# Reordering a step of an attention loop: output matmuls dealt out among scores and attention, transposes between the two value tiles

## What is computed

```python
h_q = (x @ w_q.T).reshape(b, lq, H, DH)
h_k = (key_value_states @ w_k.T).reshape(b, lk, H, DH)
h_v = (key_value_states @ w_v.T).reshape(b, lk, H, DH)
score = jnp.einsum('bqhd,bkhd->bhqk', h_q, h_k)
score = score + position_bias[None]
m = attention_mask[:, None]
score = jnp.where(m, score, -jnp.inf)
score = jax.nn.softmax(score, axis=-1)
score = jnp.where(m, score, 0.0)
attn = jnp.einsum('bhqk,bkhd->bqhd', score, h_v).reshape(b, lq, H * DH)
out = attn @ w_out.T
```

## Time and profile before

| | |
|---|---|
| runs of the kernel before | 1075.21, 1072.99, 1074.5 us; median 1074.5 |
| profiled execution: span | 1071.4 us (the page gives no other time of this execution) |
| PE busy | 1037.1 us, 97% |
| PEld busy | 903.5 us, 84% |
| DVE, ACT, POOL busy | 659.0, 458.9, 313.4 us |
| chain that ended last | PE 88%, DVE 5%, POOL 2%, ACT 2% |
| PE waiting for probabilities (line 1463) | 5.5 us, 2 times, longest 4.2 |
| PE waiting for their split (line 1336) | 4.5 us, 3 times, longest 1.6 |

### The profile page before, as it was taken

The page is one execution under the profiler, slowest core; times in us unless marked ns, Lnnn a source line. Parts: engine busy times, 40 slices in busy tenths (PEclk is TensorE's granted clock), DMA queues, the critical chain, the costliest instruction groups (busy, mean ns, idle before and its releaser), DMA issues.

```text
span 1071.4 us, 16826 instructions
## 1 busy us (share of the span) xinstructions
PE 1037.1 (97%) x5946; PEld 903.5 (84%) x5946; DVE 659.0 (62%) x1189; ACT 458.9 (43%) x1090; POOL 313.4 (29%) x236
## 2 busy tenths in 40 slices
PE   8989999999999999999999999999999999799995
PEld 7778888888888888888888888888888888578784
DVE  5766666666666666666666666666666666853615
ACT  6866343434343434343434343434343434254251
POOL 1645040404040404040404040404040402343204
PEclk9999999999999999999999999999999999899998
DMA  9402020202020202020202020202020300300011
GB/s 299 134 1 84 2 84 1 83 0 83 0 83 0 83 0 83 0 83 0 83 0 83 0 83 0 83 0 83 0 83 0 122 1 20 109 21 1 1 40 40
DMA packets 20698, 52.39 MB, mean 49 GB/s; under 512 B 3136, under 2 KB 7232, under 8 KB 20672
## 3 DMA queue, kind: packets, MB, share of 16 engines
q1 hardware_dynamic: 20672, 52.06, 14.6%
HBM read 49.95 MB, written 2.10 MB: 49 GB/s over the span
## 4 chain that ended last, share of the span: by engine, by line
PE 88%; DVE 5%; POOL 2%; ACT 2%; issue 1%; DMA 1%; DVEq 0%; SPq 0%; POOLq 0%; ACTq 0%
PE psum L1330 25%; PE psum L1332 25%; PE psum L1331 25%; PE psum L1336 8%; PE psum L1337 3%; PE psum L1463 3%; DMA raw<-in_dft 1%; POOL rows L511 1%; DVE st L1045 0%; PE psum L1568 0%; DVE wts L1012 0%; POOL stat L581 0%; DVE rsum L1240 0%; ACT xn_hi L647 0%; POOL stat L583 0%
## 5 line engine op out<-in xcount | busy, mean ns | idle before, releaser
L539 POOL TENSOR_TENSOR smx<-far,bias 128x512 f32<-128x512 f32 x64 | 82.7, 1292 | 423.2 <-DVE smx L1068 421.5
L735 ACT ACTIVATE smx<-smx,nmax 128x128 f32<-128x128 f32 x256 | 99.8, 391 | 231.8 <-DVE nmax L1074 231.8
L976 DVE TENSOR_TENSOR qk<-psum,qk 128x512 fp32r<-128x512 f32 x136 | 93.2, 687 | 105.1 <-ACT qk L647 105.1
L1330 PE MATMUL psum<-wv_lo,cx_hi 128*128 128x256 f32 x512 | 149.7, 292 | 0.3 <-DVE xn_lo L976 0.3
L1332 PE MATMUL psum<-wv_hi,cx_hi 128*128 128x256 f32 x512 | 144.5, 282 | 0.0
L1331 PE MATMUL psum<-wv_hi,cx_lo 128*128 128x256 f32 x512 | 144.5, 282 | 0.0
L647 ACT ACTIVATE qk<-psum 128x512 fp32r<-128x512 f32 x136 | 80.8, 596 | 140.7 <-PE psum L1332 140.6
L976 DVE TENSOR_TENSOR vv_lo<-psum,vv_hi 128x512 fp32r<-128x512 f32 x64 | 44.2, 691 | 124.9 <-ACT vv_hi L647 124.9
L489 POOL TENSOR_TENSOR wqk_lo<-raw,wqk_hi 128x1024 fp32r<-128x1024 f32 x31 | 74.3, 2396 | 127.8 <-ACT wqk_hi L647 127.8
L1330 PE MATMUL psum<-wo_lo,at_hi 128*128 128x512 f32 x256 | 105.9, 414 | 1.1 <-issue 1.1
L1330 PE MATMUL psum<-cx_lo,wqk_hi 128*128 128x512 f32 x256 | 100.3, 392 | 1.8 <-DVE wqk_lo L976 1.8
(11 more groups left out here) (184 smaller groups left out, 2351.7 us busy)
## 6 DMA issues: line engine op xcount, KB each, us to landing
raw<-in_wqk SPq DMA_DIRECT2D x32, 512.0 KB, 3.4
raw<-in_wv SPq DMA_DIRECT2D x16, 512.0 KB, 4.3
raw<-in_wo SPq DMA_DIRECT2D x16, 512.0 KB, 3.3
raw<-in_ffn SPq DMA_DIRECT2D x10, 512.0 KB, 3.3
raw<-in_dft SPq DMA_DIRECT2D x7, 512.0 KB, 4.6
acc<-in_x SPq DMA_DIRECT2D x2, 1024.0 KB, 9.1
raw<-in_ctxT SPq DMA_DIRECT2D x4, 512.0 KB, 10.2
bias<-in_bias SPq DMA_DIRECT2D x32, 64.0 KB, 1.8
```

What stands on the lines that cost most here:

```text
L539: nc.gpsimd.tensor_tensor(bm, far[:, HB * hf:HB * hf + HB, :], g_, ALU.add).then_inc(s_bm_ready, 1)
L735: a.activation(exps[:, b, :], scores_sb[:, b, :], ACT.Exp, bias=nmax[:, 1, b:b + 1], accum_out=esum[:, 0, b:b + 1]).then_inc(s_exp_done, 1)
L976: return v.tensor_tensor(dst, src, hi, ALU.subtract)
L1330: mm(out, lhs(0), rhs(1), start=first, stop=False)
```

## The change

PE's order in a step becomes: `project`, the first value tile, `turn_probs`, the second value tile, then the scores of step n + 1 with the six matmuls of the first output tile between them, then the attention of step n with the six of the second output tile between them. The waits of scores and of the first output bank stand ahead of the first block, those of attention and of the second bank ahead of the second. DVE follows: `softmax_in`, first `add_out`, `attended`, `softmax_out`, second `add_out`. ACT, POOL and SP keep their order. The number of instructions is the same. Step 0 keeps its order, step 1 has no outputs (its scores come ahead of its attention), step 62 has no values, step 63 is as before. `mm3` moves from lines 1330 to 1332 to lines 1333 to 1335, other lines likewise.

```diff
             every_pair(dve, pair_dve)
...
-                    attended(n, j)
                     if is_first(g) and j == 0:
+                        attended(n, j)
                         xt_lo(4)
                         xt_lo(5)
-                    if front:
                         softmax_in(n + 1)
...
+                    elif is_first(g) and j == 1:
+                        softmax_in(n + 1)
+                        attended(n, j)
+                        softmax_out(n + 1)
+                    elif last and j == 3:
+                        attended(n, j)
+                    else:
+                        softmax_in(n + 1)
+                        add_out(n - 2, 0, (2 * ((j + 2) % 4)) % B)
+                        attended(n, j)
+                        if last and j == 2:
+                            ffn_lo(UP[3])
+                        softmax_out(n + 1)
+                        add_out(n - 2, 1, (2 * ((j + 2) % 4) + 1) % B)
...
+            def scores_and_output(n, o, first_tile):
+
+                scores_ready(n)
+                output_bank(o, 0)
+                score_hi(0)
+                output_term(o, first_tile, 0, 0)
+                score_lo(0)
+                output_term(o, first_tile, 0, 1)
+                score_hi(1)
+                output_term(o, first_tile, 0, 2)
+                score_lo(1)
+                output_term(o, first_tile, 0, 3)
+                score_hi(2)
+                output_term(o, first_tile, 0, 4)
+                score_lo(2)
+                score_hi(3)
+                output_term(o, first_tile, 0, 5)
+                score_lo(3)
...
+            def attend_and_output(n, g, j, o, first_tile):
+
+                attend_ready(n, g, j)
+                output_bank(o, 1)
+                attend_hi(j, 0)
+                output_term(o, first_tile, 1, 0)
+                attend_lo(j, 0)
...
             def pair_pe(g):
...
-                    turn_probs(n)
-                    if not (last and j >= 2 or is_first(g) and j == 0):
-                        values(n + 2, g + (j >= 2), (2 * j + 4) % B)
-                    attend(n, g, j)
                     if is_first(g) and j == 0:
+                        turn_probs(n)
+                        attend(n, g, j)
                         transposes(HB)
                         transposes(HB + 1)
-                    if front:
                         scores(n + 1)
...
+                    elif last and j == 3:
+                        outputs(n - 2, g, 2)
+                        turn_probs(n)
+                        attend(n, g, j)
+                    else:
+                        if last and j == 2:
+                            turn_probs(n)
+                        else:
+                            values(n + 2, g + (j >= 2), tile)
+                            turn_probs(n)
+                            value_tile(tile, 1)
+                        if is_first(g) and j == 1:
+                            scores(n + 1)
+                            attend(n, g, j)
+                        else:
+                            outputs_ready(n - 2, g - (j < 2), tile)
+                            scores_and_output(n + 1, n - 2, tile)
+                            attend_and_output(n, g, j, n - 2, tile)
```

More of the change, by code:

```diff
@@ L1436, in values, with value_tile, score_hi, score_lo @@
                     pe.wait_ge(s_o_add, 2 * m - 8)
[L1437 to L1444, removed]
+                value_tile(first_tile, 0)
+            def value_tile(first_tile, i):
+                tk = slice((first_tile + i) * P, (first_tile + i + 1) * P)
+                for c in range(DC):
+                    last = mm3(psV[:, i * 2 * P:(i + 1) * 2 * P], lambda i_: cx[i_][:, c, tk],
+                               lambda i_: wv[i_][:, c, :], c == 0, c == DC - 1)
+                if i == 1:
+                    last.then_inc(s_v_mm, 1)
+            def score_hi(b):
+                bk = slice(b * P, (b + 1) * P)
+                mm(psS[:, b], qk[0][:, 0, bk], qk_parts[:, :, 1, bk], start=True, stop=False)
+            def score_lo(b):
+                bk = slice(b * P, (b + 1) * P)
+                last = mm(psS[:, b, 1], qk[1][:, 0, bk], qk[0][:, 1, bk], start=False, stop=True)
+                if b == HB - 1:
+                    last.then_inc(s_scores_mm, 1)
+            def scores_ready(n):
                 pe.wait_ge(s_q_lo, n + 1)
@@ L1450, in scores @@
                     pe.wait_ge(s_stats_a, HB + 1)
+            def scores(n):
+                scores_ready(n)
                 for b in range(HB):
[L1452 to L1454 removed]
+                    score_hi(b)
+                    score_lo(b)
             def turn_probs(n):
@@ L1474, in attend, with outputs_ready @@
                     pe.wait_ge(s_general, 2)
+            def attend(n, g, j):
+                attend_ready(n, g, j)
                 for b in range(HB):
[L1476 to L1480, removed]
+                    attend_hi(j, b)
+                    attend_lo(j, b)
+            def outputs_ready(o, g, first_tile):
                 hf = first_tile // HB
@@ L1488, in outputs, with output_bank @@
                     pe.wait_ge(s_a_lo, 4 * g + 2 + 2 * hf)
-                for i in range(2):
[L1490 to L1507, removed]
+            def output_bank(o, i):
+                if isinstance(o, int) and o in LATE:
+                    pe.wait_ge(s_q_lo, units)
+                    pe.wait_ge(s_k_lo, units)
+                    pe.wait_ge(s_scores_full, units)
+                    pe.wait_ge(s_o_add, 2 * (o - 2) + i + 1)
+                else:
+                    if i == 0:
+                        pe.wait_ge(s_k_lo, min(o + 4, units) if isinstance(o, int) else o + 4)
+                    else:
+                        pe.wait_ge(s_v_lo, min(o + 5, units) if isinstance(o, int) else o + 5)
+                    if isinstance(o, int) and due(2 * (o - 1) + i + 1):
+                        pe.wait_ge(s_o_add, 2 * (o - 1) + i + 1)
@@ new lines, in output_term, with outputs @@
+            def output_term(o, first_tile, i, k):
+                hf, tile, hp = first_tile // HB, (first_tile + i) % HB, k // 3
+                lhs, rhs = ((0, 1), (1, 0), (0, 0))[k % 3]
+                last = mm(out_banks(o)[i][:, :], at[lhs][:, hf, hp, tile * P:(tile + 1) * P], wo[rhs][:, hp, :],
+                          start=k == 0, stop=k == 5)
+                if k == 5:
+                    last.then_inc(s_o_mm, 1)
+            def outputs(o, g, first_tile):
+                outputs_ready(o, g, first_tile)
+                for i in range(2):
+                    output_bank(o, i)
+                    for k in range(6):
+                        output_term(o, first_tile, i, k)
```

51 lines of the change are left out of this document (30 added, 21 removed).

## The result

The changed kernel takes **1080.05 us** (median of 4 runs, 1079.42 to 1080.78) against 1073.74 us of the kernel before in the same session: a ratio of 1.0058, 95% interval 1.0041 to 1.0075. So it is slower by 0.6%, three times what can be told from no change. The forecast of 1075 us has this time in its range (1067 to 1083), but its sum missed by 5 us and the likeliest case, "same", did not happen.

What follows compares the result with a forecast made beforehand. TensorE was taken as the bound, busy 1037.1 of 1071.4 us. Terms -1.3 (step 2), 0 (loop) and +1.9 (end) summed to +0.6 us; with 3.1 us carried over from span to median, 1075 us, range 1067 to 1083.

Steps and rivals of the forecast that it cites:

- same: Whole kernel: time within 0.2% of the kernel before, given a chance of 0.47.
- The -1.3 us of step 2: Transposes between the two value tiles: the first tile fills PE's 1.29 us wait for probabilities in step 2.
- the three distances: Loop step: output add 1.25 us to spare, value split 0.8 us, key split done long before; no new wait, 0.
- loads hidden: Rival: loads behind low parts are fetched during the output before, 21.5 us less, 1053 us; chance 0.13.
- The end: Last pair of heads: last transposes move by +0.7 or +3.1 us, depending on POOL's third split; middle +1.9 taken.
- The high end: Upper range limit, 1083 us: forecast with +3.1 at the end, the clock's 4.2 us and small case of slow outputs.
- nothing in the rows decides between them: Last pair: whether DVE's next small operation precedes POOL's third split, probabilities ready at 918.2 or 920.6 us.
- the first term: Output matmuls dealt among scores and attention, 61 steps: taken as zero, at best 4.3 us less.
- the prediction's own sign: Loop step: forecast is wrong if the 13.38 us period moves by more than 0.035 us, since 61 make 0.2%.
- outputs slow beside short matmuls: Rival: dealt outputs beside 128-column matmuls cost more; 3.7 us, 1079 us, or 12.8 us, 1088 us; chance 0.18.
- the 0.235 by which I wanted to know it: Sign of slow outputs: more than 0.235 us per output matmul instead of 0.2325 us.
- The clock: Stretch at 1.2 GHz after the wait before the last transposes: 0 taken, bounds 4.2 us either way.

Runs made afterwards that it cites:

- e1: Changed kernel with the twelve output matmuls back in one piece behind attention, other reordering kept; 1072.86 us, ratio 0.999 to the kernel before.
- e5: Changed kernel with each output bank's six matmuls in one block in the middle of scores or attention; 1078.75 us, ratio 1.0059 to the kernel before.
- e2: Changed kernel with only the first output bank dealt among the scores, the second in one piece behind attention; 1073.98 us, ratio 0.9997 to the kernel before.
- e6: e1 with ACT's and POOL's weight splits at the loop's end reordered, the fourth piece moved from DVE to POOL; 1066.72 us, ratio 0.9938 to the kernel before.
- e7: Changed kernel with the new end of e6, the third piece's high part also made before the attention's copy; 1072.56 us, ratio 0.998 to the kernel before.
- e9: Changed kernel with the low parts of scores and attention 256 columns wide instead of 128; 1078.69 us, ratio 1.0039 to the kernel before.
- e4: Kernel before the change with low parts of scores and attention 256 columns wide instead of 128; 1074.9 us, ratio 1.0003.
- e8: e1 with the second value tile moved behind the attention, ahead of the outputs; PE waits in every step; 1148.72 us, ratio 1.0691 to the kernel before.
- e3: Changed kernel with the last exponentials ahead of ACT's four weight pieces, POOL and DVE splitting later; 1077.08 us, ratio 1.0024 to the kernel before.

## Why the prediction came out as it did

*Right.* The -1.3 us of step 2 came. The loop has no new wait: neither the output add nor the value split nor the keys make PE wait there, as the three distances said. No load runs more than one matmul ahead: the low part behind a 0.23 us output costs 0.10 us, so the rival "loads hidden" (1053 us) did not happen. With that the reading of the Trainium skill's "TensorE: Matmul & The Clock Gate", section "Step-by-step: what each phase is for", as loads pulled ahead to the queue's full depth is not borne out; in this kernel's rows it is one.

*Mis-sized.* The end was given as +0.7 or +3.1 us with the middle, +1.9, taken. The rows show the +3.1 end: the clamp came behind POOL's third split. The time lies in the range because the range allowed for this end and for slow outputs. The high end is added up wrongly: its terms, 1074.5 - 1.3 + 3.1 + 4.2 + 3.7, give 1084 us and not 1083, which changes nothing here. The step that could have been sharper is "nothing in the rows decides between them": in the earlier trace rows POOL's splits hold up DVE's small operation to the end of a split, and in the sum the clamp fell within the third.

*Wrong.* The step that failed is the first term, the output matmuls dealt out among scores and attention, for which the prediction takes zero: the loop gave +3.9 us. By the prediction's own sign, a period that moves by more than 0.035 us, the forecast is wrong: it moved by 0.066. It priced a matmul by its neighbours' loads alone, and read the 0.07 us by which outputs exceed projections as a property of the outputs. It is a property of the place. e1 shows that the dealing causes the loss, e5 that dealing in two blocks of six does not avoid it (half the dealing, e2, does in the loop), and the series moving from outputs to projections shows the place. What in PE makes the place slow stays open. The rows had it: in the earlier trace rows only the first distance was read, 507.27 - 507.02 = 0.25; the other eleven outputs cost (2.79 - 0.25) / 11 = 0.231 us, also more than 0.227. The rival "outputs slow beside short matmuls" (0.18) had the side, and its 1079 us is near, but that is in part luck, for it held the rest of the sum at the middle end of +1.9 us; and its mechanism is not borne out: the outputs cost 0.2335 us each instead of 0.232, below the 0.235 by which I wanted to know it; the projections behind pay.

*The clock* (+0.5 us behind the last transposes against the 0 taken) was within its bounds.

## What to carry to other kernels

Where narrow and wide matmuls alternate, price a block by its place: read the cost of each matmul by position over a whole step, before concluding that one kind is dearer. Keep the narrow ones together, so that one slow series is paid per step and not two; in this kernel the second one cost 0.5% of the step. At a loop's end, look at what stands in the queues ahead of the last softmax: moving work of ACT and POOL out of that chain was worth 6 to 8 us here (e1 to e6, changed to e7), about as much as the whole change cost (6.3 us).

## What was not expected of the hardware

- Behind matmuls of 128 or 256 columns the next wide ones run at 225 to 244 ns instead of 227: 10 of them behind scores and attention in one piece (before, e1), 11 in the changed kernel, 10 in e5, 7 in e2 and e9, 5 where all the narrow ones have 256 columns (e4), and 5 behind a wait of PE in the middle of wide ones (e8). Why, and what sets the number, stays open: no row shows what PE is short of there, and no run separated it.
- A wide matmul between narrow ones costs about 0.233 us, whether the narrow ones have 128 or 256 columns (changed, e9).
- DVE's scalings of one tensor with a small operand stall beside a POOL split until that split ends: 128x4 takes up to 2.30 us instead of 0.17, 128x512 takes 2.01 us instead of 0.54. A low part of 128x1024 with all operands in SBUF takes 2.97 us (changed) instead of 1.26 (e3). The low part of the attention, which reads PSUM, keeps 0.66 to 0.69 us beside a split (e6, at 916 us).
- The granted clock fell to 0.50 in e6 behind PE waits of only 1.47, 0.71 and 0.40 us, which ended at 912.42, 914.26 and 915.32 us.
